# Compact 16x16 inverse blocks, packed turns, and work moved between two passes of a gated-delta-rule loop

## What is computed

```python
mixed = silu(causal_conv4(x @ W_qkv, conv_w))        # width 2*2048 + 4096
q, k, v = split(mixed); q, k = l2norm(q)/sqrt(128), l2norm(k)
for t in range(T):                                    # per head: S is 128x128
    S = S * exp(g[t])
    S = S + beta[t] * outer(k[t], v[t] - k[t] @ S)
    o[t] = q[t] @ S
o = rmsnorm(o) * norm_w * silu(x @ W_z)
y = o @ W_out                                         # summed over all heads
out = x + y * silu(moe(xn))
```

## Time and profile before

| | us |
|---|---|
| median of 3 runs | 2122.12 |
| lowest and highest | 2114.63, 2125.47 |
| profiled execution | 2117.74 |
| its span, first to last instruction | 2115.8 |

### The profile page before, as it was taken

The page is one execution under the profiler, slowest core; times in us unless marked ns, Lnnn a source line. Parts: engine busy times, 40 slices in busy tenths (PEclk is TensorE's granted clock), DMA queues, the critical chain, the costliest instruction groups (busy, mean ns, idle before and its releaser), DMA issues.

```text
span 2115.8 us, 43478 instructions
## 1 busy us (share of the span) xinstructions
PE 1917.6 (91%) x15082; PEld 1402.3 (66%) x15082; DVE 1505.7 (71%) x2430; ACT 984.2 (47%) x2535; POOL 759.0 (36%) x685
## 2 busy tenths in 40 slices
PE   4578886888799999999999999999999999999998
PEld 3246662333555687877878778787687777877877
DVE  5786771111677687787787877878778787787887
ACT  1012224777213354645545455455564555645544
POOL 4730002110300334616336164362543624526343
PEclk9689998999899999999999999999999999999999
DMA  6635661000122200010010000100001001010010
GB/s 245 209 91 200 184 178 55 26 20 1 55 60 70 82 17 35 5 35 30 15 35 10 30 30 15 35 30 10 30 15 35 30 10 40 5 35 30 15 45 20
DMA packets 75254, 111.75 MB, mean 53 GB/s; under 512 B 23318, under 2 KB 56742, under 8 KB 72006
## 3 DMA queue, kind: packets, MB, share of 16 engines
q1 hardware_dynamic: 71694, 102.32, 15.1%
q0 software_dynamic: 3072, 8.39, 1.3%
q10 hardware_dynamic: 446, 0.48, 0.1%
HBM read 85.80 MB, written 28.52 MB: 54 GB/s over the span
## 4 chain that ended last, share of the span: by engine, by line
PE 51%; DVE 16%; issue 4%; ACT 3%; POOL 0%; DVEq 0%; ACTq 0%; POOLq 0%
PE ps L1273 5%; PE ps L1311 4%; PE ps L1321 4%; DVE conv L1862 3%; DVE P L2034 3%; DVE P_term L2031 3%; PE ps L1544 3%; PE ps L1493 3%; PE ps L1533 3%; PE ps L1428 3%; PE ps L1417 3%; PE ps L1546 3%; PE ps L1520 2%; PE ps L1450 2%; PE ps L1525 2%
## 5 line engine op out<-in xcount | busy, mean ns | idle before, releaser
L1862 DVE SCALAR_TENSOR_TENSOR conv<-raw,tap_st,conv 128x1024 f32<-128x1024 f32 x204 | 299.5, 1468 | 3.6
L1273 PE MATMUL ps<-xnT,w_conv_st 128*128 128x512 f32 x544 | 247.6, 599 | 0.0
L1842 POOL TENSOR_TENSOR o<-o,silu_z 128x256 f32<-128x256 f32 x128 | 138.5, 1082 | 255.5 <-DVE silu_z L1882 141.7
L816 DVE TENSOR_REDUCE m_part<-ps 128x1 f32<-128x640 f32 (+7 forms) x176 | 176.4, 1027 | 67.1 <-PE ps L667 53.5
L1726 POOL TENSOR_TENSOR gmask_Q<-upto,g 128x2048 f32<-128x2048 f32 x17 | 61.4, 3611 | 363.5 <-PE ps L1500 335.5
L998 ACT ACTIVATE probs<-ps 128x1024 f32<-128x1024 f32 (+7 forms) x256 | 145.9, 660 | 58.1 <-PE ps L933 28.7
L1273 PEld LDWEIGHTS ps<-xnT,w_conv_st 128*128 128x128 f32 x544 | 98.9, 191 | 101.1 <-issue 96.2
L1565 ACT COPY raw<-ps 128x512 f32<-128x512 f32 x136 | 80.7, 594 | 173.4 <-PE ps L1273 173.4
L1822 POOL TENSOR_TENSOR kq_decayed<-conv,decay_rows 128x1024 f32<-128x1024 f32 x64 | 159.3, 2521 | 0.0
L1321 PE MATMUL ps<-w_z_st,xnT 128*128 128x256 f32 x512 | 148.8, 393 | 0.0
L903 POOL DMA_INDIRECT slot_outputs<-scratch_slots_y,token_slots x32 | 30.6, 958 | 310.9 <-POOLq L496 202.0
(11 more groups left out here) (345 smaller groups left out, 4728.9 us busy)
## 6 DMA issues: line engine op xcount, KB each, us to landing
decay_rows<-scratch_egc SPq DMA_DIRECT2D x17, 1024.0 KB, 4.7
w_conv_st<-in_w_conv SPq DMA_DIRECT2D x17, 512.0 KB, 3.3
scratch_slots_x<-yacc SPq DMA_DIRECT2D x8, 1024.0 KB, 14.9
slot_rows<-scratch_slots_x SPq DMA_DIRECT2D x16, 512.0 KB, 4.7
scratch_slots_y<-slot_outputs SPq DMA_DIRECT2D x16, 512.0 KB, 3.4
w_gate_up<-in_gu SPq DMA_DIRECT2D x8, 768.0 KB
w_gate_up<-in_gu SPq DMA_DIRECT2D x32, 192.0 KB
kq_decayed<-in_gu SPq DMA_DIRECT2D x22, 256.0 KB, 2.8
```

The source lines that it names most:

```text
L816: dve.tensor_reduce(dst, src, AX.X, ALU.max).then_inc(s_max, 1)
L1273: mm = pe.matmul(ps[:, 6 + n % 2, :], wc[:, k, (n // 2) * P:(n // 2 + 1) * P], m.xnT[:, k, (n % 2) * HALF:(n % 2 + 1) * HALF], start=k == ...
L1842: g.tensor_tensor(oc, oc, zs[:, c, :], ALU.mult).then_inc(s_oz, 1)
L1862: op = dve.scalar_tensor_tensor(out=cv[:, t, :], in0=raw[:, t, at:at + T], scalar=tap[:, t, at:at + 1], in1=cv[:, t, :], op0=ALU.mult, op1 ...
```

## The change

Seven things are changed, all in the loop of the second layer but for the first filling:
- *Compact storage.* A block-diagonal matrix with blocks up to 64 rows is kept as 64 columns for each 128 rows: the half of the columns that is zero is left out. P is spread to 64 columns (pd) instead of 128, Q is kept so too (qd); both lie in the room of gmask_Q. Levels 4 and 5 work on 32 columns for each half-chunk instead of 64; the masks halve.
- *Packed turns.* Two chunks of 64 columns are turned in one 128x128 transpose: 4 for each e instead of 8. At the first turn and at level 5, ACT puts the result in place with four copies of a quarter each, instead of one.
- *Level 5* has its matmuls on all four 64x64 quadrants of PE (by chunk parity and half), and its results in two banks.
- *U and its mask.* ACT copies the 32-row pieces of U into a PSUM bank, DVE's mask reads them there, and the halves are added by a reduction. The start value of P is copied by ACT instead of DVE.
- *Convolution group 3* is done over two passes: (3,0) stays, (3,1) to (3,3) open the next pass on DVE, and (3,T) stands behind the gate there. POOL's copy of the taps moves from the pass's end behind kq_decayed. No conv product stands between the two masks of a level, and (1,T) comes behind the last level's copies.
- *Projections* stand one place later: four, not five, ahead of the first turn, one more in level 5.
- *The gate of the second half of the outputs* stands behind U on DVE, and PE's turns and output projections are split in two halves around kk and A1.

```diff
-                for n in range(4):
+                for n in range(2):
+                    project_out(i, n)
+                for n in range(2, 4):
                     turn_outputs(i, n)
...
-                for n in range(5):
+                for n in range(4):
                     project(i + 1, n)
 
                 for e in range(2):
                     pe.wait_ge(s_p0 if e == 0 else s_p1, i + 1)
-                    for c in range(NC):
-                        mm = pe.transpose(ps[:, 2 * e + c // 4, (c % 4) * P:(c % 4 + 1) * P], e_p[:, e, c, :], m.ident[:])
+                    for j in range(NC // 2):
+                        mm = pe.transpose(ps[:, 2 + e, j * P:(j + 1) * P], pd[:, e, 2 * j:2 * j + 2, :].rearrange("p c n -> p (c n)"), m.ident[:])
                     mm.then_inc(s_qt, 1)
-                    project(i + 1, 5 + e)
+                    project(i + 1, 4 + e)
...
-                                mm = pe.matmul(ps[h, e, c * 64:(c + 1) * 64], e_p[h, e, c, h], xs[h, e, c, :], start=True, stop=True)
+                                g, at, _, _, bank, slot = place(lv, c, h)
+                                mm = pe.matmul(ps[h, bank + base(lv, e), slot * 32:(slot + 1) * 32], pd[g, e, at, :], xs32[g, e, at, :], start=True, stop=True)
                         mm.then_inc(s_y, 1)
-                    if lv == FIRST:
-                        project(i + 1, 7)
+                    project(i + 1, 6 + lv - FIRST)
...
+                tanh_conv(i, 3)
+                for n in range(2):
                     turn_out(i, n)
+                nc.scalar.copy(pc[:], eye1[:].unsqueeze(1).broadcast_to([P, UNITS, BLK])).then_inc(s_ch, 1)
                 act.wait_ge(s_u, i * 4 + 4)
...
-                    nc.scalar.copy(u32[rows].rearrange("p u t i -> p u (t i)"), uu[rows, :, rows]).then_inc(s_u32, 1)
+                    nc.scalar.copy(ps[rows, U_BANK, :].rearrange("p (u n) -> p u n", u=UNITS), uu[rows, :, rows]).then_inc(s_u32, 1)
...
-                    nc.scalar.copy(chunks(gm_q[:, e]), two_banks(2 * e)).then_inc(s_q, 1)
-                    copy_raw(i + 1, 5 + e)
+                    for h, odd, src in halves(e):
+                        last = nc.scalar.copy(qd[h, e, odd::2, :], src)
+                    last.then_inc(s_q, 1)
+                    copy_raw(i + 1, 4 + e)
...
-                g.tensor_tensor(e_p[:, 1].rearrange("p c (b i) -> p c b i", i=BLK),
-                                pc[:, NC:, :].unsqueeze(2).broadcast_to([P, NC, NB, BLK]),
-                                bmask[:].unsqueeze(1).unsqueeze(3).broadcast_to([P, NC, NB, BLK]), ALU.mult).then_inc(s_p1, 1)
+                g.tensor_tensor(pd[:, 1].rearrange("p c (b i) -> p c b i", i=BLK),
+                                pc[:, NC:, :].unsqueeze(2).broadcast_to([P, NC, NB // 2, BLK]),
+                                bmask4[:].unsqueeze(1).unsqueeze(3).broadcast_to([P, NC, NB // 2, BLK]), ALU.mult).then_inc(s_p1, 1)
...
-                dve.tensor_tensor(uc[:], u32[:, :, 0, :], u32[:, :, 1, :], ALU.add).then_inc(s_uc, 1)
-                add_out(i, 3)
+                dve.tensor_reduce(uc[:], u32[:].rearrange("p u t i -> p u i t"), AX.X, ALU.add).then_inc(s_uc, 1)
+                for n in range(1, 4):
+                    add_out(i, n)
 
                 n = 1
-                dve.tensor_copy(pc[:], eye1[:].unsqueeze(1).broadcast_to([P, UNITS, BLK])).then_inc(s_ch, 1)
...
-                        + [(1, TAPS)] + [(2, k) for k in range(TAPS)] + [(3, 0), (3, 1), (2, TAPS), (3, 2), (3, 3), (3, TAPS)])
+                        + [(2, 0), (1, TAPS), (2, 1), (2, 2), (2, 3), (3, 0), (2, TAPS)])
```

More of the change, by code:

```diff
@@ L1202, in sc, with place, halves, base @@
             return scal[:, NAMES[name], e, c:c + 1]
+        def place(lv, c, h):
+            j, hi = c // 2, int(h is HI)
+            if lv == FIRST:
+                return h, c, 0, c, 0, c
+            return (LO, HI)[c % 2], 2 * j + hi, hi, j, c % 2, j
+        def halves(e):
+            turned = ps[:, 2 + e, :].rearrange("p (j h n) -> p j h n", h=2, n=64)
+            return [(h, odd, turned[(LO, HI)[odd], :, int(h is HI), :]) for h in (HI, LO) for odd in range(2)]
+        def base(lv, e):
+            return (e, (4, 0)[e], (4, 1)[e])[lv - FIRST]
         def chunks(ap):
@@ L1684, in _ @@
                     if e == 0:
-                        if lv == FIRST + 1:
-                            tanh_conv(i + 1, 1)
-                        if lv == FIRST:
-                            copy_raw(i + 1, 7)
+                        copy_raw(i + 1, 6 + lv - FIRST)
                     act.wait_ge(s_t, i * NT + n + 1)
-                    nc.scalar.copy(chunks(e_p[:, e]), two_banks(2 + 2 * e)).then_inc(s_pt, 1)
+                    if lv == FIRST:
+                        nc.scalar.copy(chunks(pd[:, e]), ps[:, 2 + e, :]).then_inc(s_pt, 1)
+                    else:
+                        for h, odd, src in halves(e):
+                            last = nc.scalar.copy(e_p[h, e, odd::2, h], src)
+                        last.then_inc(s_pt, 1)
+                tanh_conv(i + 1, 1)
                 tanh_z(i, 0)
@@ L1795, in _ @@
             totals(0)
-            pool.wait_ge(s_conv, 4)
-            passed()
-            g.tensor_copy(tap[:], m.taps[:, 1]).then_inc(s_taps, 1)
-            pool.wait_ge(s_dve, 5)
+            pool.wait_ge(s_dve, 7)
             passed()
@@ L1844, in _ @@
                         rsqrt_outputs(i, c // 4)
-                pool.wait_ge(s_conv, i * 4 + 8)
-                passed()
-                g.tensor_copy(tap[:], m.taps[:, bass.ds(i + 2, 1), :, :].rearrange("p a b c -> p (a b) c")).then_inc(s_taps, 1)
         @block.vector
```

112 lines of the change are left out of this document (68 added, 44 removed).

## The result

| | before | after |
|---|---|---|
| median of 5 runs | 2122.12 | 2135.56 |
| lowest and highest | 2114.63, 2125.47 | 2131.94, 2137.47 |
| profiled execution, its span | 2117.74, 2115.8 | 2133.62, 2131.7 |
| mean granted clock | 0.976 | 0.960 |

The ratio after to before is 1.0067 (95% interval 1.0047 to 1.0088): 13 us slower, against the 28 forecast.

What follows compares the result with a forecast made beforehand. PE was taken to bound the kernel, held at joints by DVE and POOL excluding each other. 16 x (0.57 + 1.3) - 0.6 = +29.3 on 2117.74 gives 2147, plus 3: 2150 us; range 2105 to 2176, narrower 2136 to 2168.

Steps and rivals of the forecast that it cites:

- Step 1: POOL's kq_decayed products: taking turns with DVE's conv products and gate, they end at about 1167 instead of 1162.85.
- Step 2: PE up to the row matmuls of U16: same matmuls in another order, nothing holds them, start at 1159.7, -1.0 us.
- the lock: DVE instructions reading two SBUF tensors and POOL instructions exclude each other; those with a PSUM input run at full speed.
- Steps 3 and 4: Inverse steps slowed by POOL, spread of P +1.3 to +1.9 us; PE, with four covering projections, idles 3.7 to 4.3.
- Step 5: Turns and projections 4 and 5: level 4 starts at 1179.9 to 1180.5, before 1179.88; the quarter copies cost nothing.
- Step 6: Levels 4 and 5: matmuls priced as before, 6.8 us per level, 13.6 in all against 15.06, -1.5.
- a rival with a chance of 0.08: Level 5 on four quadrants running at once: X and QX halve, -2 per pass, 2118 us; chance 0.08.
- Step 7: Behind the last level: gmask_Q on POOL delays (1,T), PE waits; 8.0 us to W instead of 6.0, +2.0.
- Step 8: Recurrence: W starts +0.55 to +1.1, 0.25 comes back at S; without the clock +0.3 to +0.85 per pass.
- Step 9: Granted clock falls with PE's long wait in each pass: at most 1.66 us, 0.8 if half lies in it, 1.3 taken.
- Step 10: Outside the loop: the last pass saves one unused conv product, -0.6 us; MoE units and masks at the start give nothing.

Runs made afterwards that it cites:

- e1_term_psum: Kernel of after with the product of each inverse step kept in PSUM instead of SBUF; ratio to before 0.9816.
- e6_five_ahead: Kernel of after with five projections ahead of the first turned P instead of four, none in level 5; ratio to before 0.9952.
- e4_quadrants: Kernel of after with level 5's matmuls reordered by diagonal pairs of quadrants; ratio to before 1.0175.
- e10_one_quadrant: Kernel of after with level 5's matmuls reordered to four in a row on one quadrant, then the next; ratio to before 1.0177.
- e12_both_filled: Kernel of after with unread matmuls filling both PE waits, ahead of the turned P and ahead of turn_kq; ratio to before 0.9947.
- e3_filled: Kernel of after with four unread matmuls filling PE's first wait, ahead of the turned P; ratio to before 1.0071.
- e2_mask_later: Kernel of after with gmask_Q on POOL waiting until DVE's (1,T) is done; ratio to before 1.0088.
- e11_all: Kernel of after with convolution group 3 in one pass again, the inverse steps' term in PSUM and gmask_Q behind the last group-2 tap; ratio to before 0.9869.
- e8_both: Kernel of after with the inverse steps' term in PSUM and gmask_Q moved into a gap of the recurrence; ratio to before 0.9591, 1999.5 us.

## Why the prediction was right in the time, and where its steps failed

*Step 1, POOL: right in kind, 1.7 too late.* kq_decayed ends 23.8 us into the pass; I had 25.5, before it was 21.3.

*Step 2, U16 and the rows: held.* The forecast counted 0.69 to 1.2 for the reduction and no wait for POOL. No row of before that it rests on shows a reduction of one SBUF tensor beside POOL; in after it takes 0.70 beside kq_decayed (1084.15), so this one stays out of the lock. The rows start 17.8 us into the pass (18.2 forecast), PE is through at 29.8 (30.2). But the reading that the lock takes two SBUF tensors is too narrow, and the trace of before already had a case against it: the first tap, with one SBUF tensor, takes 2.42 us instead of 0.75 beside POOL's spread of P (L1860 at 1174.41).

*Steps 3 and 4: held in kind, each a little under its range.* Two subtractions of 2.11 and 1.99, the spread 0.9 later than before (1.3 to 1.9 forecast), PE's wait 3.59 (3.7 to 4.3). e1_term_psum shows the cause, e6_five_ahead the missing cover. *Step 5:* level 4 starts 38.1 us into the pass, before 38.35; the quarter copies cost at most the 0.21 that PE waits for the last of them.

*Step 6, the two levels: the term that was mis-sized.* I wrote 13.6 for them and it was 12.15 (before 15.06). I priced level 5 at the pace of one pair of quadrants and left four of them to a rival with a chance of 0.08. This rival held: X and QX take 1.14 instead of 2.06, 1.8 less per pass, of which 0.5 comes back as the wait for X. That four run at once no run of before shows. The only row I had was for two quadrants, and it already showed them side by side, 64 records in 2.08 against 32 in 2.07 on one; nothing in the trace spoke for a halt at two. 0.08 was far too little. That the order sets the pace (e4_quadrants, e10_one_quadrant) shows that it is the quadrants and not the narrower columns.

*Step 7: held.* 8.0 from the last level to W, 8.0 forecast. (1,T) took 3.10 and not 4.5, since it started late, behind ACT's tanh; the wait is the same, because gmask_Q's end sets it. *Step 8:* 0.16 came back, 0.25 forecast.

The sum without the clock was to be +0.3 to +0.85 per pass; it was -1.29. Of the distance to the middle, 1.9, step 6 is 1.45, and the rest is step 3, whose spread of P came 0.7 earlier than the middle of its range, less 0.3 in small terms.

*Step 9, the clock: right in its mean, wrong in its form.* 1.3 per pass were taken, 1.5 were measured: two falls in every second pass, not one in each. The 1.66 that capped the price of a fall is 5.38 less 3.72 us for 16 records of L1311 behind the loop, the first with 3.4 us at 0.50 behind a wait of 1.62, the second at 1.00 (2106.9 to 2110.3). Before has no wait over 0.95 us in the steady passes and so does not show what one of 4 us does there; in after, from the third pass on, the clock fell in every second pass only. e12_both_filled shows it whole, and that both waits do it. I had taken the second, of 2 us, as good for at most 0.4; e3_filled shows it lowering the clock to 0.50 in each pass by itself.

*Step 10, outside the steady passes: this failed.* I wrote -0.6. The first two passes cost 10.2 more than before. I built one pass in the middle of the loop and multiplied by 16; in the first one DVE and POOL stand otherwise to each other. Another 3.0 lie ahead of the loop, where the start of the loop varies by up to 8 us among kernels of one chip, so I assign them to nothing.

So 16 x 1.87 became 13 passes that add 1.2 together, and 14.7 us elsewhere (10.2 in the first two, 3.0 ahead of the loop, 1.4 in the last stretch). The forecast that PE would wait and the clock would fall was right; the sign of the steady pass at full clock was not. That the time fell into the range is luck: two errors of opposite sign, step 6 and step 10. The ends of the narrower forecast were also added up from two different starting values; from 2117.74, with the 0.6 and the 3 us of the middle value, they are 2138 and 2167.

## What to carry to other kernels

Where DVE and GpSimd work side by side, keep one operand of each short DVE step of a chain in PSUM, even an intermediate that DVE itself writes; here that single line took two steps from 2.11 and 1.99 us to 0.40 and 0.39 and was worth 2.5% (e1_term_psum). A long GpSimd product had no cheap place next to DVE taps here, only a gap with few of them: moving it a little only picked another victim (e2_mask_later: PE waits 1.94 us for S instead of 1.95 for (1,T)). Where instructions of both engines become ready together, look at every pass: a tie within 0.03 us decided over 1.6 us of PE (e11_all). Price waits of PE by what they do to the clock as well: filling one of two gave nothing (e3_filled, 1.0071), and removing both gave more than the sum of the single edits (e8_both, 100 us against 53 and 27). And lay out the first pass of a software-pipelined loop by itself.
